# The quantised network's tiles set between the attention's steps, twelve steps per tile

## The reference

```
# attention: 16 heads, keys of 64 compressed columns, per graph
q, k   = projections of layernorm(x) and of the roped context
attn   = softmax(q k^T);  x = x + (attn @ kv) @ P      # P, N: weights folded beforehand

# quantised network
s   = 127 / max|x_row|;   xq = clip(round(x * s)) / s      # x here is layernorm(x)
x1, x3 = split(xq @ w13)                                # 2 * 704 columns
g   = relu(x1)^2 * x3
h   = g * rsqrt(mean(g^2) + eps) * norm_w
s2  = 127 / max|h_row|;   hq = clip(round(h * s2)) / s2
x   = x + hq @ w2                                       # 704 -> 256
```

## Time and profile before

| | before |
|---|---|
| median of 3 runs | 578.06 us (577.68 to 578.91) |
| the profiled execution's own time | 578.1 us |
| its span, first to last instruction | 576.3 us |
| TensorE busy | 482.9 us (84%) |
| VectorE, ScalarE, GpSimd busy | 370.3, 257.9, 206.5 us |
| mean granted TensorE clock | 0.936 |
| start of attention, of the network | about 321 and 494 us |

### The profile page before, as it was taken

How to read it: one execution, slowest core, us unless ns; L and a number is a source line. 1 busy time by engine, 2 the same in 40 slices (tenths; PEclk the granted TensorE clock), 3 DMA queues, 4 the chain that set the end, 5 groups by cost and what they waited for, 6 DMA issues and landing times.

```text
span 576.3 us, 9861 instructions
## 1 busy us (share of the span) xinstructions
PE 482.9 (84%) x3261; PEld 323.7 (56%) x3268; DVE 370.3 (64%) x1093; ACT 257.9 (45%) x654; POOL 206.5 (36%) x278
## 2 busy tenths in 40 slices
PE   3798888887728999999797899999999977978785
PEld 2455556555514844675356567767767744644553
DVE  5799898889665950231858565365365387388872
ACT  1477566657313521322111456356356355235652
POOL 1215245455342000931776243243243243213221
PEclk9999799999867999999987799999999998988995
DMA  9980000000050050894347000000000000000000
GB/s 219 325 173 2 1 3 1 3 1 1 2 150 1 2 175 1 246 277 128 97 101 85 7 1 2 2 0 2 1 2 1 1 1 1 1 2 18 10 19 28
DMA packets 28370, 30.15 MB, mean 52 GB/s; under 512 B 4673, under 2 KB 26402, under 8 KB 28066
## 3 DMA queue, kind: packets, MB, share of 16 engines
q1 hardware_dynamic: 25554, 24.74, 15.5%
q0 software_dynamic: 1536, 4.20, 3.9%
q10 hardware_dynamic: 1232, 0.60, 0.4%
HBM read 26.38 MB, written 3.15 MB: 51 GB/s over the span
## 4 chain that ended last, share of the span: by engine, by line
PE 58%; DVE 19%; issue 9%; ACT 7%; POOL 5%; DMA 2%; ACTq 0%; DVEq 0%; POOLq 0%
PE bank L819 5%; PE bank L764 5%; PE bank L846 5%; PE bank L868 4%; DVE work L1414 4%; PE bank L834 4%; PE bank L858 4%; DVE work L1407 3%; PE bank L778 3%; PE bank L936 3%; PE bank L589 3%; PE bank L558 2%; PE bank L796 2%; PE bank L906 2%; PE bank L956 2%
## 5 line engine op out<-in xcount | busy, mean ns | idle before, releaser
L1918 POOL TENSOR_SCALAR work<-work,R 128x256 f32<-128x256 f32 x128 | 58.9, 478 | 75.9 <-DVE R L1651 75.9
L1193 ACT ACTIVATE work<-bank,nmx 128x256 f32<-128x256 f32 x128 | 58.9, 472 | 56.6 <-DVE nmx L1639 56.5
L1407 DVE CUSTOM_DVE_ANT_0 work<-bank,Nw 128x256 f32<-128x256 f32 x128 | 46.5, 418 | 10.0 <-PE bank L575 9.9
L1414 DVE TENSOR_SCALAR work<-work,M 128x256 f32<-128x256 f32 x128 | 50.0, 452 | 0.0
L1639 DVE TENSOR_REDUCE nmx<-bank 128x2 f32<-128x512 f32 x64 | 41.3, 686 | 11.4 <-PE bank L846 11.1
L846 PE MATMUL bank<-work 64*128 64x256 f32 x256 | 43.8, 419 | 3.1 <-ACT work L1193 3.0
L1058 ACT ACTIVATE work<-bank 128x512 f32<-128x512 f32 x64 | 35.1, 604 | 19.4 <-PE bank L589 19.1
L1909 POOL DMA_INDIRECT arena<-eout,idx x32 | 32.1, 1002 | 30.9 <-DMA eout<-work 21.5
L858 PE MATMUL bank<-arena,kvb 128*64 128x256 f32 x256 | 36.1, 402 | 7.2 <-DVE arena L1630 7.0
L1051 ACT ACTIVATE bank<-bank 128x512 f32<-128x512 f32 x64 | 35.0, 597 | 9.0 <-PE bank L575 9.0
L834 PE MATMUL bank<-ident,work 128*128 128x128 f32 x256 | 35.4, 284 | 2.2 <-POOL work L1918 2.0
(11 more groups left out here) (223 smaller groups left out, 990.1 us busy)
## 6 DMA issues: line engine op xcount, KB each, us to landing
work<-in_wg SPq DMA_DIRECT2D x16, 176.0 KB, 3.7
work<-in_wu SPq DMA_DIRECT2D x16, 176.0 KB, 4.0
work<-in_wd SPq DMA_DIRECT2D x16, 176.0 KB
arena<-in_wq SPq DMA_DIRECT2D x1, 2048.0 KB, 10.3
arena<-in_woT SPq DMA_DIRECT2D x1, 2048.0 KB, 17.2
eout<-work SPq DMA_DIRECT2D x16, 128.0 KB, 3.3
arena<-in_kcqT SPq DMA_DIRECT2D x1, 1536.0 KB, 21.4
arena<-in_w13T SPq DMA_DIRECT2D x1, 1408.0 KB, 7.9
```

The lines of the kernel that those rows point to most:

```text
L1193: act.activation(E2[:, j % 2, t, h, :], bank[h][:, t * S:(t + 1) * S], ACT.Exp, bias=nmx[:, j % 2, h, t:t + 1], accum_out=S2[:, j % 2, h, ...
L1407: dve.tensor_tensor_reduce(L[:, i % 4, t, :], bank[XB[i % 4]][:, t * S:(t + 1) * S], maskN[:, g, t, :], 1.0, -3.4e38, ALU.add, ALU.max, M[ ...
L1414: dve.tensor_scalar(L[:, i % 4, t, :], L[:, i % 4, t, :], M[:, i % 4, t:t + 1], None, ALU.subtract).then_inc(d_ready, 1)
L1918: pool.tensor_scalar(E2[:, j % 2, t, h, :], E2[:, j % 2, t, h, :], R2[:, j % 2, h, t:t + 1], 1.0, ALU.mult, ALU.mult).then_inc(en2_ready, 1)
```

## The change

Tiles 0 to 5 of the quantised network are cut into pieces `i` and placed between the attention's steps: `ff_steps(s)` gives for each tile `n` the piece of step `s`, `i = s - 9 - 8 (n // 2) - 3 (n % 2)`. Pieces: 2 `ff_first`; 3 in-transposes; 4, 5, 6 the three chunks of `ff_in`; 5, 6, 7 relu, square and gate of each; 7 sum of squares and weighing; 8 mean and largest; 9 root and `ff_second`; 10 integers; 11 back transposes; 12 `ff_out`; 13 `ff_result`. A pair of tiles takes 8 steps, the second tile 3 steps behind. So tile 0 starts in step 11 and tile 5 in step 30. What is left of tiles 4 and 5, and tiles 6 and 7 in full, stand behind the attention.

`ff_in` is 18 matmuls of 512, 512 and 384 columns, each with equal parts of both halves, for 24 of 512 and 192. All chunks of tiles 0 to 5 share bank 6, and transposes and output of a tile share bank 7. To free these, the attention keeps one bank (4) for the context, where it had two; queries, transposed rows and output of later graphs use bank 5; two query pairs share a bank and one copy. VectorE's statistics stand behind the reciprocal, those for graphs 2 and 3 two steps earlier than before. TensorE waits for the split weights before step 2. The hardware loops go.

```diff
+        CHUNKS = ((0, 256), (256, 256), (512, HID - 512))
+
+        def in_bank(n, c):
+            return bank[6] if n < NT - 2 else bank[(3 * (n - NT + 2) + c) % 5]
+
+        def query_bank(b, i):
+            return bank[5 if b else 6 + i % 2]
+
+        def side_bank(n):
+            return bank[7 if n < NT - 2 else 6 if n == NT - 2 else 5]
+
+        def ff_steps(s):
+
+            return [(s - 9 - 8 * (n // 2) - 3 * (n % 2), n) for n in range(NT - 2)]
+
         block = ctx.enter_context(nc.Block())
 
...
+            def att_queries(b, i):
...
+                pe.wait_ge(q_evac, b * 4 + i + 1 if b else max(i, 1))
+                for j in (2 * i, 2 * i + 1):
+                    for k in range(KT):
+                        mm = pe.matmul(query_bank(b, i)[:, j % 2 * S:(j % 2 + 1) * S], Nw[:, k, j * P:(j + 1) * P],
+                                       xT3[:, k, :], start=k == 0, stop=k == 1)
                 mm.then_inc(q_mm, 1)
...
+            def ff_in(n, c):
+
+                lo, w = CHUNKS[c]
...
+                if n < NT - 2 and n + c > 0:
+                    pe.wait_ge(f_g_ready, 3 * n + c)
+                if n >= NT - 2 and c == 0:
+                    pe.wait_ge(x3_ready, B + 1)
+                if n == NT - 1 and c == 2:
+                    pe.wait_ge(f_g_ready, 3 * n - 2)
+                i = 0
+                for part in range(3):
+                    for k in range(KT):
+                        both = w13p[:, part, k, :].rearrange("p (u n) -> p u n", u=2)
+                        mm = pe.matmul(in_bank(n, c)[:, 0:2 * w].rearrange("p (u n) -> p u n", u=2),
+                                       q1T[:, n % TB, k * P:(k + 1) * P], both[:, :, lo:lo + w],
+                                       start=i == 0, stop=i == 5)
+                        i += 1
                 mm.then_inc(f_a_mm, 1)
...
-                    att_back_transposes(b, j - 2)
-                    att_scores(b, j)
-                    att_context(b, j - 2)
-                    if j == 3:
...
-                att_output(b)
-            for j in range(2, AH // 2 + 2):
-                att_back_transposes(B - 1, j - 2)
...
-            ff_in(0, 0)
-            att_output(B - 1, last=True)
-            ff_in(1, 1)
-
...
-            with pe.Fori(1, B - 1) as b:
-                for t in range(TB):
-                    ff_back_transposes(b * TB + (t - 1), 1 - t)
-                    ff_in(b * TB + (t + 1), 1 - t)
-                    ff_out(b * TB + (t - 1), 1 - t)
-                    ff_in_transposes(b * TB + (t + 2), t)
...
+            for s in range(2, B * 8 + 2):
+                b, j = divmod(s, 8)
+                att_back_transposes((s - 2) // 8, (s - 2) % 8)
+                if b < B:
+                    att_scores(b, j)
+                for i, n in reversed(ff_steps(s)):
+                    if i == 3:
+                        ff_in_transposes(n)
+                    elif i == 11:
+                        ff_back_transposes(n)
+                att_context((s - 2) // 8, (s - 2) % 8)
+                if j == 3 and b < B - 1:
+                    att_ln_transposes(b + 1)
+                if j >= 4 and b < B - 1:
+                    att_queries(b + 1, j - 4)
+                if j == 1 and b > 0:
+                    att_output(b - 1, last=b == B)
+                for i, n in ff_steps(s):
+                    if 4 <= i <= 6:
+                        ff_in(n, i - 4)
+                    elif i == 12:
+                        ff_out(n)
+
+            ff_in(NT - 3, 2)
+            ff_back_transposes(NT - 4)
+            ff_out(NT - 4)
+            ff_in_transposes(NT - 2)
+            for c in range(3):
+                ff_in(NT - 2, c)
+            ff_in_transposes(NT - 1)
+            for c in range(3):
+                ff_in(NT - 1, c)
+            for n in (NT - 3, NT - 2, NT - 1):
+                ff_back_transposes(n)
+                ff_out(n)
+
...
+            def ff_relu(n, c):
...
+                act.wait_ge(f_a_mm, 3 * n + c + 1)
+                act.activation(r1[:, lo:lo + w], in_bank(n, c)[:, 0:w], ACT.Relu,
+                               scale=is1[:, n % TB:n % TB + 1]).then_inc(f_relu, 1)
+                act.wait_ge(f_relu, 3 * n + c + 1)
+                act.activation(r2[:, lo:lo + w], r1[:, lo:lo + w], ACT.Square).then_inc(f_r_ready, 1)
...
+            for s in range(2, B * 8 + 2):
+                b, j = divmod(s, 8)
+                for i, n in ff_steps(s):
+                    if 5 <= i <= 7:
+                        ff_relu(n, i - 5)
+                att_back_evac((s - 2) // 8, (s - 2) % 8)
+                if b < B:
                     att_exp(b, j)
-                    if j == 3:
-                        att_ln_evac(b + 1)
...
+                for i, n in ff_steps(s):
+                    if i == 7:
+                        ff_square(n)
+                    elif i == 10:
+                        ff_integers(n)
+                for i, n in reversed(ff_steps(s)):
+                    if i == 3:
+                        ff_in_evac(n)
+                    elif i == 11:
+                        ff_back_evac(n)
+                if j == 3 and b < B - 1:
+                    att_ln_evac(b + 1)
+                if j >= 4 and b < B - 1:
+                    att_query_evac(b + 1, j - 4)
+
+            ff_relu(NT - 3, 1)
+            ff_integers(NT - 4)
+            ff_relu(NT - 3, 2)
+            ff_square(NT - 3)
+            ff_back_evac(NT - 4)
+            ff_in_evac(NT - 2)
+            for c in range(3):
+                ff_relu(NT - 2, c)
+            ff_in_evac(NT - 1)
+            ff_integers(NT - 3)
             ff_square(NT - 2)
-            ff_back_evac(NT - 3, 1)
-            ff_relu(NT - 1, 1)
-            ff_integers(NT - 2, 0)
+            ff_back_evac(NT - 3)
+            for c in range(3):
+                ff_relu(NT - 1, c)
+            ff_integers(NT - 2)
             ff_square(NT - 1)
-            ff_back_evac(NT - 2, 0)
-            ff_integers(NT - 1, 1)
-            ff_back_evac(NT - 1, 1)
+            ff_back_evac(NT - 2)
+            ff_integers(NT - 1)
+            ff_back_evac(NT - 1)
+
...
+            def ff_gate(n, c):
+
+                lo, w = CHUNKS[c]
+                dve.wait_ge(f_r_ready, 3 * n + c + 1)
+                if n > 0:
+                    dve.wait_ge(f_sq_ready, n)
+                    dve.wait_ge(f_w_ready, n)
+                dve.scalar_tensor_tensor(gated[:, lo:lo + w], in_bank(n, c)[:, w:2 * w], is1[:, n % TB:n % TB + 1],
+                                         r2[:, lo:lo + w], ALU.mult, ALU.mult).then_inc(f_g_ready, 1)
...
+            for s in range(2, B * 8 + 2):
+                b, j = divmod(s, 8)
+                att_back_evac((s - 2) // 8, (s - 2) % 8)
+                for i, n in ff_steps(s):
...
                     att_max(b, j)
-                    att_context_evac(b, j - 2)
-                    if j == 2:
-                        layernorm_stats(b + 1, base2, l2_veps)
-                    if j == 3:
...
+                att_context_evac((s - 2) // 8, (s - 2) % 8)
+                if b < B:
                     att_inverse(b, j)
...
+                if j == (0 if b else 2) and b < B - 1:
+                    layernorm_stats(b + 1, base, l2_veps)
+                if j == (1 if b else 3) and b < B - 1:
+                    dve.wait_ge(l2_T_mm, b + 1)
+                    att_ln_apply(b + 1)
+                if j == 1 and b > 0:
+                    if b < B:
+                        att_keys(b)
+                    att_add(b - 1)
+                if j == 2 and b > 0:
+                    dve.wait_ge(x3_ready, b + 1)
+                    layernorm_stats(b - 1, base, f_veps, keep_at=b - 1)
+                for i, n in ff_steps(s):
+                    if i == 2:
+                        ff_first(n)
+                    elif i == 8:
+                        ff_mean(n)
+                        ff_largest(n)
+                    elif i == 9:
+                        ff_second(n)
+                    elif i == 13:
+                        ff_result(n)
+            ff_second(NT - 4)
+            ff_gate(NT - 3, 1)
             dve.wait_ge(x3_ready, B + 1)
             layernorm_stats(B - 1, base, f_veps, keep_at=B - 1)
-            base += steps[0]
-            FF_STEPS = 27
-            with dve.Fori(1, B - 1) as b:
-                base3 = b * FF_STEPS + (base - FF_STEPS)
-                steps[0] = 0
-                for t in range(TB):
-                    n = b * TB + t
-                    ff_gate(n, t, base3)
-                    ff_result(b * TB + (t - 2), b - 1, t)
-                    ff_first(b + 1, t, base3)
-                    ff_first_integers(b * TB + (t + 2), t, base3)
-                    ff_mean(n)
-                    ff_largest(n, base3)
-                    ff_second(n, t, base3)
-                assert steps[0] == FF_STEPS, steps[0]
-            base += (B - 2) * FF_STEPS
-            steps[0] = 0
```

(64 more changed lines are left out.)

310 lines of the change are left out of this document (83 added, 227 removed).

## The result

The changed kernel takes 598.3 us (median of 4 runs, 597.54 to 600.92); the kernel before took 577.87 (577.33 to 578.91) beside it. The ratio is 1.0359, with a 95% interval of 1.0322 to 1.0396. I had forecast 589, slower, with a range up to 598. The direction was right; the time lies 0.3 us above the range.

What follows compares the result with a forecast made beforehand. Bound by TensorE's work plus waits on VectorE's round: 510.0 bare plus 31.6 of waits gives 541.6; tail 44 makes 585.6; clock and port terms 2 make 587.6; 1.8 around the span gives 589 us, 8-in-10 range 569 to 598.

Steps and rivals of the forecast that it cites:

- The mechanism: Attention steps: whatever VectorE does behind its reciprocal is added in full to the round, and TensorE's context product waits.
- the wait of step 19: TensorE idle ahead of the context product, from scores done to VectorE's evacuation, some 3.5 us.
- my two refuting signs: Wrong if the last output ends before 530 us, or ScalarE rather than VectorE releases most context products.
- Waits in the attention: Place-by-place count from step 8 to the last output at 541.6 us: 31.6 us of waits over the bare 510.0.
- the clock term: Lower TensorE clock after idling in steps 19 and 27: bounds 0 and 3 us, taken as 1.
- The sign that I gave: Expected in the changed profile: mean clock above 0.936.
- The port lock: VectorE's `ff_first` held beside GpSimd's weighing in steps 19 and 27: bounds 0 and 2.6 us, taken as 1.
- The round of 3.6 us: VectorE, one reciprocal to the next: evacuation 0.7, two maxima 1.3, wait for ScalarE's exponentials 1.5, reciprocal 0.2.
- The tail: Work behind the last attention output, through tiles 6 and 7 to the final store: 44 us.
- The holes are filled: Rival: TensorE's chunks run inside former waits, giving 562 us; filled or half-filled together had chance 0.24.
- half-way case: Partly filled holes: 20 us of waits and a tail of 42, giving 574 us; chance 0.24 shared with fully filled.
- The clock falls: Rival: clock stays low in second and third graph; steps 19, 20, 27, 28 cost 7 us more, 596; chance 0.10.

Runs made afterwards that it cites:

- e2_pieces: Changed kernel with VectorE's statistics, scaling and the network's VectorE pieces ahead of the reciprocal; ratio to the kernel before 1.0019.
- e4_onepart: Changed kernel leaving out two of three weight parts of the input products of tiles 0 to 5; ratio to the kernel before 1.0202.
- e11_early: Kernel before with only VectorE's statistics and scaling of the next graph's rows moved behind the reciprocal; ratio to the kernel before 1.0207.
- e3_weigh: Changed kernel with GpSimd's weighing ahead of the normalising of the same step; ratio to the kernel before 1.0189.
- e8_warm: Changed kernel with 39 idle matmuls added where TensorE waits for VectorE; ratio to the kernel before 1.0334.
- e10_warm2: Changed kernel with 31 idle matmuls, sized by their measured price, where TensorE waits; ratio to the kernel before 1.0301.
- e7_tail: Changed kernel with statistics and network pieces ahead of the reciprocal, weighing ahead of normalising, and work behind the last output reordered; ratio to the kernel before 0.9890.

## Why the prediction was right in direction and short in size

- *The mechanism* was right: VectorE's round sets the light steps. Steps 10 to 12 came in 14.3 us (forecast 14.45), 13 to 15 in 18.44 (18.45), the wait of step 19 was 3.19 (3.5), and e2_pieces and e4_onepart bear it out. Of my two refuting signs neither showed: the last output ended at 553.7, not before 530, and ScalarE releases 2.3 us of the context product's waits against VectorE's 12.6.
- *The failed step*, first part: the start of "Waits in the attention". I counted from 358.0, the start of step 8 in the kernel before, as if the edit of the statistics began there. It also acts in steps 2 and 3 of graph 0: 3.7 us that the sum put at nothing. e11_early shows how far I had under-sized this edit by itself: 12 us, where my terms make 3.
- *The failed step*, second and larger part: the clock term, taken as 1 with 3 as its bound. Outputs 1 and 2 (+1.6, +1.7), the queries of step 20 (+1.4) and the output product of step 32 (3.73 us for 2.23, +1.5) make 6.2. I had the earlier trace rows in hand, a context product of 1.94 us behind 2.54 of idling, and charged only the places of the longest waits. Where the low clock falls is partly chance: in the four other traces with the changed order in graph 0 (e3_weigh, e4_onepart, e8_warm, e10_warm2) output 1 was at full clock and graph 0, from the first to the eighth reciprocal, took 37.8 us instead of 36.7. The sign that I gave was wrong as well: the mean clock is 0.934, not above 0.936.
- *The gate waiting for the weighing* (steps 17 and 25) was charged nothing: 9.5 us to output 2 became 10.8, and 10.4 to output 3 became 10.8. I had named what is queued behind a gate, not what it waits for.
- *The port lock* was 1 for two places; it took 1.35 at each, 2.7, just above my bound (2.6). Here was the nearest row after all: the last operation of `ff_first` does meet the weighing.
- *A reading.* The 1.5 us in which VectorE "waits for ScalarE's exponentials" hold its context copy (0.42 us) as well; the wait itself is the 0.96 of the earlier trace rows. The round of 3.6 us, on which the sum rests, is read rightly.
- *The tail*: 41.8 for 44. In the seven other traces with this order of the tail it was 40.8 to 45.0, mean 43.5, so 44 was well sized, and the 2.2 that made up for part of the miss were luck. One difference is the clock: the product of tile 4 took 2.24 us in the changed kernel and 4.13 in e3_weigh, whose tail was 44.6.
- *Together*, stage by stage in us; the differences add up to the 9.9 by which the span (595.5) exceeds 585.6:

| stage | forecast | measured | difference |
|---|---|---|---|
| start of step 8 | 358.0 | 361.7 | +3.7 |
| steps 8, 9, output 1 | 16.2 | 17.6 | +1.4 |
| steps 10 to 12 | 16.4 | 16.2 | -0.2 |
| steps 13 to 15 | 18.4 | 18.4 | 0 |
| steps 16, 17, output 2 | 16.7 | 19.6 | +2.9 |
| steps 18 to 20 | 20.6 | 22.8 | +2.2 |
| steps 21 to 23 | 21.8 | 21.0 | -0.8 |
| steps 24, 25, output 3 | 17.5 | 17.9 | +0.4 |
| steps 26 to 33, output 4 | 56.0 | 58.5 | +2.5 |
| tail | 44.0 | 41.8 | -2.2 |

- *The rivals.* "The holes are filled" is false as the change was made; the same instructions in another order come near its half-way case of 574 (e7_tail, 572). "The clock falls", at 596 and a chance of 0.10, was nearest, in part by luck: of its 7 us in steps 19, 20, 27 and 28 only the 1.4 of step 20's queries shows in the terms above. A clock term of that size should have been part of the forecast, since it follows from the very waits I forecast.

## What to carry to other kernels

Before pieces go between the steps of a loop, find the instruction on each engine that waits longest for another engine, and put them ahead of it. Behind it the same instructions are paid in full in every round that this engine sets, and here that alone made 19.7 us. A wait of TensorE is to be charged up to twice where it is as long as here (1.7 to 2.5 us), for what stands behind it may run at 1.2 GHz. Take the wait away rather than fill it: filler gave some 3.3 us by the ratios both times, with overlapping intervals, and a slow stretch that goes at one place can come back at the next wait. When an edit of this kind is priced, every place where it acts counts, also those ahead of the part that the change is about.

## What the runs showed of the hardware

- A float32 matmul of 256 columns with its weight load takes 0.45 to 0.5 us at full clock (four in 1.99 us), so 0.22 per record of the trace.
- The granted clock went with the idle time ahead: output 2 took 8.72 to 10.02 us behind 2.4 to 2.6 us of idling (granted 0.71 to 0.82) and 7.07 to 7.17 with the wait filled or gone (1.00). A single place is not certain. Tile 4's output product took 2.24 us behind 2.33 of idling in the changed kernel (granted 1.00) and 4.13 behind 2.32 in e3_weigh (0.50); output 1 took 8.80 behind 1.27 and 0.52 in the changed kernel and 7.17 behind the same in e3_weigh.
- A VectorE operation of 0.29 us took 1.64 beside GpSimd's weighing and 0.29 again when the two no longer met. By the Trainium skill, "SBUF — State Buffer", who interferes with whom, VectorE in a two-port mode and GpSimd contend for a shared port pair, and whichever issues first holds it for its whole instruction. The trace agrees: the weighing runs from 449.11 to 450.81, and the operation that started at 449.32 ends at 450.96.
